# A recurrent layer on one core: the moving operand of each weight tile is streamed once instead of twice

## The reference

```python
z  = sigmoid(xz[t] + h @ U_z + vz)
r  = sigmoid(xr[t] + h @ U_r + vr)
hh = tanh(xh[t] + (r * h) @ U + vh)
h  = (1 - z) * h + z * hh          # out[t] = h
```

## Time and profile before

| | before |
|---|---|
| median of 3 runs | 5869.0 us |
| profiled execution | 5866.45 us, its span 5864.7 us |
| TensorE matmul busy | 5728.9 us (98%) |
| TensorE weight load busy | 5628.1 us (96%) |
| VectorE busy | 5322.7 us (91%) |
| ScalarE busy | 4185.8 us (71%) |
| mean granted TensorE clock | 0.996 of full speed |

### The profile page before, as it was taken

How to read it: one execution, slowest core, us unless ns; L and a number is a source line. 1 busy time by engine, 2 the same in 40 slices (tenths; PEclk the granted TensorE clock), 3 DMA queues, 4 the chain that set the end, 5 groups by cost and what they waited for, 6 DMA issues and landing times.

```text
span 5864.7 us, 509556 instructions
## 1 busy us (share of the span) xinstructions
PE 5728.9 (98%) x200328; PEld 5628.1 (96%) x200328; DVE 5322.7 (91%) x47287; ACT 4185.8 (71%) x29549; POOL 8.3 (0%) x32
## 2 busy tenths in 40 slices
PE   8999999999999999999999999999999999999999
PEld 8999999999999999999999999999999999999999
DVE  6999999999999999999999999999999999999998
ACT  3777777777777777777777777777777777777776
POOL 0000000000000000000000000000000000000000
PEclk8999999999999999999999999999999999999999
DMA  3000000000000000000000000000000000000000
GB/s 93 22 20 20 22 20 22 22 18 22 20 22 20 22 18 22 21 22 20 20 22 20 22 22 18 22 20 22 20 22 18 22 21 22 20 20 22 20 22 20
DMA packets 80764, 133.66 MB, mean 23 GB/s; under 512 B 12336, under 2 KB 18480, under 8 KB 80304
## 3 DMA queue, kind: packets, MB, share of 16 engines
q1 hardware_dynamic: 80304, 129.81, 6.4%
HBM read 20.46 MB, written 8.65 MB: 5 GB/s over the span
## 4 chain that ended last, share of the span: by engine, by line
PE 88%; DVE 9%; issue 2%; ACT 0%; DVEq 0%; POOL 0%; POOLq 0%
PE quad L298 53%; PE pair_z L298 26%; PE ps_p L261 9%; DVE quad L577 3%; DVE h_part L621 2%; DVE z_fac L613 1%; DVE z_fac L607 1%; DVE rh_part L595 0%; ACT r_term L411 0%; DVE pair_z L577 0%; PE pair_z L249 0%; DVE h_fac L644 0%; DVE h_safe L647 0%; DVE oT L651 0%; DVE y_next L543 0%
## 5 line engine op out<-in xcount | busy, mean ns | idle before, releaser
L298 PE MATMUL quad<-h_part,u_part 128*128 128x48 f16 (+1 forms) x65568 | 2048.0, 183 | 108.4 <-DVE h_part L621 103.1
L298 PEld LDWEIGHTS quad<-h_part,u_part 128*128 128x128 f16 x65568 | 1854.0, 96 | 204.0 <-DVE h_part L621 151.6
L298 PE MATMUL quad<-rh_part,u_part 128*128 128x48 f16 (+1 forms) x65536 | 1998.5, 182 | 0.1
L298 PE MATMUL pair_z<-h_part,u_part 128*128 128x48 f16 (+1 forms) x65552 | 1940.2, 182 | 0.0
L577 DVE TENSOR_REDUCE quad<-quad 128x2 f32<-128x4 f32 (+1 forms) x12290 | 1881.1, 167 | 62.5 <-PE quad L298 9.4
L298 PEld LDWEIGHTS quad<-rh_part,u_part 128*128 128x128 f16 x65536 | 1847.8, 96 | 2.7 <-ACT quad L394 0.2
L298 PEld LDWEIGHTS pair_z<-h_part,u_part 128*128 128x128 f16 x65552 | 1785.1, 96 | 0.0
L621 DVE TENSOR_TENSOR_SCAN h_part<-z_fac,n_term 128x20 f16<-128x20 f32 x8192 | 1509.5, 196 | 8.3 <-issue 8.3
L419 ACT ACTIVATE n_term<-quad 128x4 f32<-128x4 f32 x8192 | 1359.7, 173 | 103.1
L411 ACT ACTIVATE r_term<-quad 128x8 f32<-128x8 f32 x4098 | 580.1, 184 | 1191.4 <-DVE quad L577 1191.4
L394 ACT ACTIVATE quad<-xp 128x8 f32 (+2 forms) x6146 | 1040.5, 183 | 30.9 <-issue 28.5
(11 more groups left out here) (80 smaller groups left out, 1942.3 us busy)
## 6 DMA issues: line engine op xcount, KB each, us to landing
w_stage<-w_in SPq DMA_DIRECT2D x384, 256.0 KB, 2.3
x_tok<-in_x SPq DMA_DIRECT2D x68, 128.0 KB, 2.6
out_dram<-o_tok SPq DMA_DIRECT2D x66, 128.0 KB, 2.3
mlp_w<-in_L_cond_W SPq DMA_DIRECT2D x2, 1024.0 KB, 6.9
u_raw<-in_L_cond_U_r SPq DMA_DIRECT2D x1, 1024.0 KB, 5.9
u_raw<-in_L_cond_U_z SPq DMA_DIRECT2D x1, 1024.0 KB, 7.9
u_raw<-in_L_cond_U SPq DMA_DIRECT2D x1, 1024.0 KB, 10.7
w_in<-in_L_cond_W_r SPq DMA_DIRECT2D x4, 256.0 KB, 10.0
```

Of the source, the lines that this page charges most:

```text
L298: return nc.tensor.matmul(to, u_part[:, g, part, k, m * P:(m + 1) * P], parts[:, at:at + run].unsqueeze(1).broadcast_to([P, repeats, run]) ...
```

## The change

One constant changes. `WIDE` is also in `cols` (its offset `at + WIDE - RUN` goes from `at + 24` to `at`) and in `tile` (`repeats` goes from 2 to 1, and the output is 24 columns from `at`). The closing tiles, the weight loads, the semaphores and all instructions of the other engines keep their number, order and size; seeds and sums use other PSUM columns of the same banks.

```diff
     RH_STEP, RH_HIGH, H_STEP, H_HIGH, AGAIN = 7, 2, 10, 5, 4
-    RUN, WIDE = 24, 48
+    RUN, WIDE = 24, 24
```

## The result

| | before | after |
|---|---|---|
| median | 5868.41 us (5865.66 to 5869.28, 4 runs) | 6518.68 us (6516.36 to 6519.76, 4 runs) |
| ratio | | 1.1108, 95% interval 1.109 to 1.1126 |
| mean granted TensorE clock | 0.996 | 0.51 |
| forecast | | 6370 us, range 6050 to 6590 |

The kernel is 11% slower. The direction and the mechanism are as forecast; the loss is 650 us where 501 were worked out.

The account below looks back on a forecast made before the run. TensorE's tile pace and VectorE's chain were taken to bound the kernel together. At the low clock, 404 us (1536 projection steps), 77 (512 others) and 20 (turns) make 501 on 5869: 6370 us, range 6050 to 6590.

Parts of the forecast that it names:

- What bounds the kernel: Recurrence step of 2.78 us: TensorE's queue, at 25.0 ns a tile, and the chain through VectorE end together.
- Unchanged clock: 0: Tiles at full clock: 24 columns less move no start, since 48 columns (20.0 ns) lie under the 25.0 ns pace.
- The gain of up to 82 us: Four places a step where TensorE resumes after a wait: at most 10 ns each, 0.04 us x 2048; taken as 0.
- The clock falls: Recurrence: with 2248 columns a step the granted clock mostly stays at 0.50; 6200 to 6600 us, chance 0.70.
- (a) Tiles: All 96 tiles of a step: 26.7 ns at the low clock instead of 25.0, 0.163 us a step.
- (b) Projection: The two float32 matmuls of a step with a projection: 0.31 to 0.46 us at the low clock, +0.15.
- (c) Stalls: Short waits in R and H of steps with a projection: the 0.07 us mostly go, -0.05 us.
- (d) Latency: The 512 steps without a projection: closing tiles +20 ns where VectorE's chain ends last; +0.15 us a step in all.
- (e) Turns: Block turns: 33 x 8 transposes at +0.11 us, 29 us, about half beside VectorE; +15 to 20 us.
- the clock stays: Rival for the recurrence: clock stays at 2.4 GHz and nothing changes, 5869 us (5860 to 5880); chance 0.13.
- it goes up and down: Rival for the recurrence: projections and transposes raise the clock, plain steps let it fall; 5900 to 6300 us, chance 0.15.
- the low level is dearer: Rival for the tiles: weight loads or issue follow the clock, 40 to 50 ns a tile, 8.8 to 10.8 ms; chance 0.02.

Follow-up runs that it names:

- kernel 3: Against the kernel before, only the candidate's (H's) unclosed tiles keep 48 columns, those of R and Z stream 24; 5875.9 us, ratio 1.0015.
- kernel 6: Against the kernel before, every tile streams only the 20 (R, Z) or 14 (H) columns that hold values; 6518.93 us, ratio 1.1107.

## Why the prediction was right, and where its size was off

**What bounds the kernel.** Right. TensorE's pace and VectorE's chain end together: leaving the projection out of 1152 steps gave nothing (5867.96 us), and at the low clock each projection cost 0.254 us at once.

**Unchanged clock: 0.** Right. 48 of 88 tiles thick gave 0.9995 at clock 0.996, and Z took 0.80 us with 24 columns where the changed kernel had its full clock. The gain of up to 82 us that the prediction allowed for resumed tiles didn't come: with all of R thin and the full clock, R took 0.85 us as before (kernel 3).

**The clock falls.** Right, and shown by experiment: the same 24 columns in the old place give 6515 us at 0.51; 12 thick tiles keep 0.974. That a gapless TensorE isn't enough, read from the 2-column matmuls of the earlier trace rows, holds over the whole recurrence: 98% busy at 0.51. One ground of the prediction didn't come true: it took the clock to be at 0.50 when the recurrence starts and to stay there. In the changed kernel the first two steps ran at the full clock, and it fell in the third (columns as in the earlier trace rows):

```profile
77.30:83.90 6.60, 6.31 (x217) 6.00 (x218) 4.98 (x45) 3.88 (x29) 0.00 (x0) 1.00 0.21 66
84.10:120.00 35.90, 35.38 (x1113) 34.58 (x1110) 30.83 (x264) 23.57 (x164) 0.00 (x0) 0.50 0.04 13
```

So the thin tiles don't only fail to raise the clock, they lose it. The prediction weighed the advice of the Trainium skill (TensorE: Matmul & The Clock Gate, "Why this matters for your kernels") to leave no long idle gaps. This trace doesn't agree with it as a sufficient condition: 98% busy at 0.51.

**(a) Tiles.** Right: Z takes 0.85 us as forecast, 26.7 ns a tile for 25.0, and kernel 6 shows the floor for tiles that follow each other directly. The penalty formula of the Trainium skill (TensorE: Matmul & The Clock Gate, "Terms") would have doubled the stretch, by the prediction's estimate; the span grew by 11%.

**(b) Projection: the term that was mis-sized.** Forecast 0.31 to 0.46 us, measured 0.31 to 0.56, on average 0.308 to 0.566: +0.26 in place of +0.15, which is 166 us in 1536 steps and so the whole error. Here are the two records of one step one by one, the first pair from the kernel before, the second from the changed one (the next R starts at 3004.41 and 3004.42):

```profile
3004.10 0.36 PE L261 MATMUL ps_p<-y_next,w_stage 128*128 128x128 f32 x1
3004.30 0.28 PE L261 MATMUL ps_p<-y_next,w_stage 128*128 128x128 f32 x1
...
3003.85 0.56 PE L261 MATMUL ps_p<-y_next,w_stage 128*128 128x128 f32 x1
3004.21 0.42 PE L261 MATMUL ps_p<-y_next,w_stage 128*128 128x128 f32 x1
```

I priced both records at the 0.22 us of the four transposes of the earlier trace rows. That fits the second one, 0.21 us to R's start (0.11 before). The first takes 0.36 us to the second's start and took 0.20 before. That is more than the 0.12 us of the dense row already at the full clock, which could have warned me. Multiplying the pair's own time by the ratio of the dense rows, 0.31 us x 0.22 / 0.12, gives 0.57 us, but I found this after the result; with the 0.11 us between the starts in the earlier trace rows it would be 0.62. In the changed kernel the mean of the projection's weight load grew from 188 to 311 ns, so part of what I had treated as streaming may be weight loading; what sets the 0.36 us was not tried by itself.

**(c) Stalls.** Right in size: the average step with a projection leaves 2.797 - 96 x 0.025 - 0.308 = 0.09 us before and 3.176 - 96 x 0.0267 - 0.566 = 0.05 us after, -0.04 for the -0.05 of the forecast. What is left is no wait for h. R takes 0.90 us for 32 x 26.7 = 0.85, because its second tile starts late after the float32 work: in this timeline of the changed kernel the two first R tiles alone take 0.25 us between the first one's start and the second one's end, at some 180 ns a tile.

```profile
3004.42 0.25 PE L298 MATMUL quad<-h_part,u_part 128*128 128x24 f16 x2
```

**(d) Latency and the steps without a projection.** Forecast +0.15, measured +0.12. Part of this is the latency of a closing tile: forecast +20 ns from four tiles of the first step, while H's closing tiles went from 168 to 173 ns over the whole trace, +5. **(e) Turns.** With the steps between the two groups of transposes (d) and (e) come to 68 us together, where 77 and 20 were forecast.

Together: +166 for the projection, +13 for tiles and stalls (187 us measured, 174 forecast) and -29 for (d) and (e) make, to the rounding, the 149 us by which the forecast was short. The projection's miss is a little larger than the whole one, because the others partly cancel.

**The rivals.** That the clock stays is refuted by the digits and by the stretches in which it was up and fell. That it goes up and down is right only at the turns: 0.51 is hardly above 0.50. That the low level is dearer is refuted by kernel 6. I had argued that projections and transposes might push the clock up. Outside the turns, where only projections are, it never came up; it did shortly after four dense transposes with 24 columns in the tiles around them, and didn't with 20 and 14 (kernel 6).

## What to carry to other kernels

Read the granted clock beside the busy shares: a TensorE that is 98% busy may be issuing short matmuls at its floor and be granted half its clock, and columns streamed into unread PSUM can hold the clock up for nothing as long as they stay under the pace of issue (here 48 columns at a pace of 25 ns, while 72 cost 21%). Before padding is removed as waste, and before it is added, try two or three doses: the effect is a step, and a few thick tiles may be enough, though near the step the clock dips for short stretches, most of them at the stalls of a turn. To price a stretch at the other clock level, don't take the absolute time of a denser row. Look first whether the stretch and that row take the same time at the clock where you have both; here the first record of the projection took 0.20 us and the dense row 0.11 to 0.12.

## What the runs showed of the hardware

- Short fp16 tiles (weight load and matmul) pace at 25.0 ns at 2.4 GHz (up to 48 columns) and 26.7 ns at 1.2 GHz, with 14, 20 or 24 columns alike. Halving the clock costs such a stream 7%.
- At 2.4 GHz a tile of 72 columns paces at 32.5 ns on average, 2.5 above its streaming; at 1.2 GHz one of 48 goes by the 40.0 ns of its columns.
- The granted clock sat at either level under almost the same work: the kernel with 2248 columns a step ran at 0.50 but for a short stretch behind the float32 transposes of most turns, the one with 1728 at 0.50 with no such rise, the one with 2536 at 1.00 but for stretches of up to 10 us, most of them about a turn. What lies between 2248 and 2536 was not tried.
- Float32 work of 128 columns is what the lower clock hurts: the projection's two records went from 0.31 to 0.56 us, 396 of the 650 us.
